# Projections of a four-layer graph network as three fp32r products each, with the head stack in three slots

## The chip, the cores and the metric

One core of one Trainium2 chip runs the whole program. The metric is the device time of one execution in microseconds (us); lower is better. Times come from repeated executions of the same program; the trace comes from one profiled execution.

## The reference, cut to what matters

For each of 32 graphs (512 nodes, 256 features) four residual layers follow one another. Each begins with `h = relu(layernorm(x))`.

```python
# layer 0:  x += silu(rmsnorm((eps*h + adj@h) @ W1 + b1) * w) @ W2 + b2
# layer 1:  hW = h@W + b; att = sigmoid(s1_i + s2_j + c) * adj, masked, rows divided by their sum
#           x += att @ hW
# layer 2:  q, k, v = h@Wq.T, h@Wk.T, h@Wv.T                   (8 heads of 32)
#           scores = q k^T / sqrt(32) + w_head * adj, -inf where adj == 0
#           x += softmax(scores) v @ Wo.T
# layer 3:  x += (D^-1/2 adj D^-1/2) @ (h @ W3) + bias
```

The change concerns the products with Wq, Wk, Wv, Wo (layer 2) and W3 (layer 3), all 256x256, 512 rows per graph.

## The kernel before, in words

`phases(t, tf)` is written once per engine. One round works on two graphs at a time: the front half (layers 0 and 1) of graph `tf = t + 1` and the back half (layers 2 and 3) of graph `t`. So there is a first round with a front half alone, 31 rounds with both halves (t = 0 to 30, 30 of them in a loop), and a last round with a back half alone. The order of the work on each engine is written out by hand; engines meet at semaphores, and each engine runs its list strictly in order, so an instruction that waits holds up all that stands behind it.

Order on TensorE (PE) in a round: `turn(t, 0)` transposes the normed features hb of the back graph (L1059), ACT and DVE copy one half each to bT (L517, L796, both called `turned`); `project_qk(t, 0, 0)` and `(t, 0, 1)` make Q and K of heads 0 to 3 (L1078); `project_v(t, 0)` half of V (L1090); `aggregate(tf)` the adjacency product of layer 0 (L958), which waits for hf, the normed input of the front graph: DVE `stats0` (L667), POOL (L340 to L346), ACT L442. Then `project_v(t, 1)`.

Then follows the grid, g = -4 to 31. At each g PE makes one score tile (L1104 and the mask product L1105, two PSUM banks in turn, so tile i waits for `biased` of tile i-2), the work of the front graph's four node tiles that `tile_steps(g)` says (tile n at its own step u = g + 4 - 8n: `hidden` at u = 0, 1; `turn_hidden` L981 at u = 5, 6; `down` L929 to L931 at u = 11 to 14, all at u = 8 for the last tile), and one group of four transposes of probabilities (L1114). At g = Q1_STEP (0) and K1_STEP (3) stand `project_qk(t, 1, 0)` and `(t, 1, 1)` (heads 4 to 7, into PSUM bank VB, L1078). One step later ACT takes the high part (L526, `qk_high`) and DVE the low part (L801, L621, `qk_low`), both at the end of that step. DVE per step: `bias` (L815), then front work (`hidden` L713 at u = 3, `silu` L719 at u = 4, 5, `hidden_lo` L621 at u = 6, 7), then at g % 4 == 1 a copy (L824). ACT per step: front work (`square` L475 at u = 1, 2, `tanh` L482 at u = 4, 5, `hidden_hi` L430 at u = 6, 7), `exps` (L536), `turned_probs` (L545).

SP copies four pieces per head from qk to a slot of `qk_stack` (`stack`, four slots, L264); head h waits for the scores of head h-4. After the grid: `attend` (L1129); `turn1(tf)` (L1003); `project_o` (L1147), which waits for `attended` on DVE (a copy L838 and a product L841, both into bT); `linear(tf)`; `turn(t, 1)` and again `turned`; `support` (L1154 to L1161, into PSUM, scaled to SBUF by ACT L551 alternating with the sigmoid L512); `attend1(tf)` (L1039, DVE L755 feeds it, `update1` L768 to L777 takes it up); `aggregate3` (L1172), DVE `update3` (L856) into x_out, and SP stores x_out.

A three-product form exists already for W1 and W2: `hi` on ACT rounds a tensor to fp32r (L430), `lo` on DVE subtracts it from the original (L621), and `product` (L926 to L931) issues hi\*hi, hi\*lo, lo\*hi. The projections above are single fp32 matmul calls.

```python
Q1_STEP, K1_STEP = 0, 3                       # L206
if b and g == K1_STEP + 1: qk_low(t, 1, 1)    # DVE; qk_high on ACT likewise
elif u in (4, 5): silu(tf, n, u - 4)          # DVE, after bias(t, g + 4)
```

## Time and profile before

| what | value |
|---|---|
| times of three runs | 4105.31, 4110.77 (median), 4115.6 us |
| span of the profiled execution, first to last instruction | 4105.1 us |
| the profiled execution's own time | not given apart from its span; the fastest run lies 0.2 us above it |
| TensorE clock granted, mean | 0.986 of full speed |
| PE busy 3772.7 us, DVE 2585.8, ACT 2302.1, POOL 688.4 | 92%, 63%, 56%, 17% of the span |

In the trace, an fp32 matmul call appears as two MATMUL rows, an fp32r or bf16 call as one. The duration of a single MATMUL contains its latency, and matmuls overlap, so the cost of one in a stream is the distance between starts. "Idle" in square brackets is time of that engine just before the instruction, and its releaser.

### The profile page before, as it was taken

The page shows a single profiled execution, that of the slowest core. Times are in us where ns is not written, and L with a number is a line of the kernel's source. Part 1 is how long each engine was busy: PE and PEld are TensorE (multiplying, and loading weights), DVE is VectorE, ACT ScalarE, POOL GpSimd, SP SyncE. Part 2 cuts the span into 40 slices and gives each one's busy share as a digit, 9 for nine tenths or more (in the row PEclk, how much of TensorE's full clock was granted, in tenths as well). Part 3 has the DMA queues.
Part 4 walks back from the last instruction along what each step waited for, and adds up shares of the span by engine and source line. Part 5 has one row for each costly group of instructions (what it writes and reads, how often), then busy time and mean ns, then how long its engine had stood idle before and what let it go on. Part 6 is the DMA issues. An engine that isn't in the chain of part 4 may idle for free.

```text
span 4105.1 us, 69147 instructions
## 1 busy us (share of the span) xinstructions
PE 3772.7 (92%) x20364; PEld 2683.0 (65%) x20364; DVE 2585.8 (63%) x6404; ACT 2302.1 (56%) x5155; POOL 688.4 (17%) x1483
## 2 busy tenths in 40 slices
PE   4899999999999999999999999999999999999997
PEld 3666666666666666766666666667666666666674
DVE  3666666666666666666666666666666666666664
ACT  2555565555665555665555655556655556555564
POOL 1121111111111211111121111121111211111110
PEclk9999999999999999999999999999999999999999
DMA  2232222222222322222222223222223222232212
GB/s 73 57 83 62 64 70 61 73 77 67 62 61 62 82 62 68 65 67 66 79 65 62 61 62 82 62 72 61 72 62 82 62 62 61 62 82 66 72 47 62
DMA packets 166933, 275.03 MB, mean 67 GB/s; under 512 B 23906, under 2 KB 59874, under 8 KB 166756
## 3 DMA queue, kind: packets, MB, share of 16 engines
q1 hardware_dynamic: 166756, 273.45, 25.3%
q14 instruction: 161, 1.32, 0.1%
q8 instruction: 16, 0.26, 0.0%
HBM read 122.37 MB, written 16.78 MB: 34 GB/s over the span
## 4 chain that ended last, share of the span: by engine, by line
PE 60%; issue 19%; DVE 11%; ACT 5%; POOL 4%; DVEq 0%; SPq 0%; DMA 0%; POOLq 0%; ACTq 0%
PE turn L1114 9%; PE value L1129 6%; PE front L929 5%; PE front L931 5%; PE front L930 5%; PE score L1104 4%; PE score L1105 4%; PE front L1039 3%; PE front L1024 3%; PE score L1147 3%; PE front L981 3%; POOL small L342 2%; PE score L1161 2%; DVE small L792 2%; DVE hid L719 2%
## 5 line engine op out<-in xcount | busy, mean ns | idle before, releaser
L536 ACT ACTIVATE prob<-prob,small 128x512 f32<-128x512 f32 x1024 | 736.3, 719 | 446.5 <-DVE small L815 445.2
L815 DVE CUSTOM_DVE_ANT_0 prob<-score,adj_sb,drv 128x512 f32<-128x512 f32 x1024 | 761.8, 747 | 250.0 <-PE score L1105 240.4
L1114 PE MATMUL turn<-ident,prob 128*128 128x128 f32 x4096 | 617.2, 276 | 14.1 <-ACT pT L545 8.3
L1114 PEld LDWEIGHTS turn<-ident,prob 128*128 128x128 f32 x4096 | 484.0, 141 | 135.7 <-issue 45.7
L545 ACT ACTIVATE pT<-turn 128x512 f32<-128x512 f32 x768 | 447.1, 585 | 140.7 <-PE turn L1114 140.6
L1104 PE MATMUL score<-qk_stack 128*128 128x512 f32 x1024 | 486.9, 479 | 20.7 <-DVE small L815 19.1
L1105 PE MATMUL score<-unlinked,neg_mask 128*128 128x512 bf16 x1024 | 399.8, 390 | 0.0
L929 PE MATMUL front<-w_hi,s_hi 128*128 128x256 f32 x1024 | 352.2, 344 | 28.5 <-DVE x_in L732 28.5
L442 ACT ACTIVATE hb<-x,small 128x256 f32<-128x256 f32 x256 | 132.8, 589 | 355.7 <-POOL small L346 355.7
L931 PE MATMUL front<-w_hi,s_lo 128*128 128x256 f32 x1024 | 287.4, 281 | 0.0
L930 PE MATMUL front<-w_lo,s_hi 128*128 128x256 f32 x1024 | 286.8, 280 | 0.0
L442 ACT ACTIVATE hf<-x_in,small 128x256 f32<-128x256 f32 x256 | 132.7, 589 | 253.1 <-POOL small L346 253.1
L929 PEld LDWEIGHTS front<-w_hi,s_hi 128*128 128x128 f32 x1024 | 196.5, 192 | 114.1 <-issue 52.6
L713 DVE SCALAR_TENSOR_TENSOR hid<-front,small,rmsw_b 128x512 f32<-128x512 f32 x256 | 180.3, 746 | 121.6 <-POOL small L365 121.6
L958 PE MATMUL front<-adjT_f,hf 128*128 128x512 f32 x512 | 228.2, 599 | 27.5 <-ACT hf L442 27.5
L1129 PE MATMUL value<-pT,vals 128*32 128x512 f32 x2048 | 252.9, 600 | 0.0
L1039 PE MATMUL front<-pT 128*128 128x258 f32 x1024 | 243.5, 389 | 6.3 <-DVE pT L755 1.6
L1078 PE MATMUL score<-bT,ws 128*128 128x512 f32 x256 | 152.4, 751 | 94.3 <-DVE bT L796 93.5
L361 POOL TENSOR_TENSOR small<-small 128x1 f32<-128x1 f32 x128 | 24.9, 195 | 1272.6 <-ACT aside L475 1272.6
L1172 PE MATMUL score<-vals,prob 128*128 128x256 f32 x1024 | 234.6, 382 | 3.3 <-ACT vals L551 0.7
L381 POOL TENSOR_TENSOR inv_x<-small,drv 128x128 f32<-128x128 f32 x256 | 94.9, 403 | 784.6 <-DVE small L831 784.6
L1039 PEld LDWEIGHTS front<-pT 128*128 128x128 f32 x1024 | 189.7, 190 | 54.8 <-DVE x L777 17.6
(137 smaller groups left out, 7515.7 us busy)
## 6 DMA issues: line engine op xcount, KB each, us to landing
qk_stack<-qk SPq DMA_DIRECT2D x1024, 128.0 KB, 2.4
adjT_f<-in_adjT SPq DMA_DIRECT2D x32, 1024.0 KB, 5.4
adj_sb<-in_adj SPq DMA_DIRECT2D x32, 1024.0 KB, 7.9
prob<-in_adjT SPq DMA_DIRECT2D x32, 1024.0 KB, 5.3
x_in<-in_x SPq DMA_DIRECT2D x32, 512.0 KB, 3.5
out<-x_out SPq DMA_DIRECT2D x32, 512.0 KB, 3.0
pT<-in_W SPq DMA_DIRECT2D x2, 1024.0 KB
rmsw_b<-in_rmsw SPq DMA_DIRECT2D x1, 512.0 KB
```

The lines of the kernel that those rows point to most:

```text
L442: act.activation(dst[:, n, :], src[:, n, :], ACT.Relu, bias=nb[:, n:n + 1], scale=rstd[:, n:n + 1]).then_inc(norm["ready"], 1)
L536: act.activation(prob[:, i % 8, :], prob[:, i % 8, :], ACT.Exp, bias=nmax[:, h, n:n + 1], scale=-1.0, accum_out=prsum[:, h, n:n + 1]).then ...
L545: act.activation(pT[:, h % HG, j, :], TB[k % 2][:, :], ACT.Copy).then_inc(pT_act, 1)
L815: dve.tensor_tensor_reduce(out=prob[:, i % 8, :], in0=SB_[i % 2][:, :], in1=adj_sb[:, n, :], scale=neg_w[:, h:h + 1], scalar=3e38, op0=ALU ...
L929: pe.matmul(ps, a[0], b[0], start=start, stop=False)
L930: pe.matmul(ps, a[0], b[1], start=False, stop=False)
L931: return pe.matmul(ps, a[1], b[0], start=False, stop=stop)
L1039: last = pe.matmul(FB[n % 2][:, 0:DE], att[:, m, tile(n)], lin[:, m, :], start=(m == 0), stop=(m == NT - 1))
L1104: pe.matmul(SB_[i % 2][:, :], qk_stack[:, h % 4, 0, tile(n)], qk_stack[:, h % 4, 1, :], start=True, stop=False)
L1105: pe.matmul(SB_[i % 2][:, :], neg_mask[:, h, :], unlinked[:, n, :], start=False, stop=True).then_inc(sc_ps, 1)
L1114: last = pe.transpose(TB[k % 2][:, tile(n)], prob[:, (4 * h + n) % 8, tile(j)], ident[:, :])
L1129: last = pe.matmul(VB[HD * h:HD * h + HD, :], vals[:, j, P * g + HD * h:P * g + HD * h + HD], pT[:, h, j, :], start=(j == 0), stop=(j == N ...
```

## The change

Wq, Wk, Wv, Wo and W3 are held as ws_hi and ws_lo (fp32r), made once at the start. bT becomes bT_hi and bT_lo. `turned` no longer splits the copy between ACT and DVE: ACT rounds both halves, DVE subtracts for both. The attention output is multiplied into a new tile o_f, then rounded by ACT (`attended_high`) and subtracted by DVE (`attended_low`). All products with these operands are three fp32r matmul calls. Q and K of heads 0 to 3 are made in one function that begins when the high part of half 0 is there. To make room, qk_stack has three slots instead of four (head h waits for the scores of head h-3), x_out lies over qk (so `qk_high` of the next graph waits for the store), inv_x and o_f lie over hb, and the widened copy wa is replaced by a broadcast view. Q1_STEP and K1_STEP go from 0 and 3 to 2 and 5. `support` makes its four tiles one after the other.

```diff
         w1_hi, w1_lo = (sb(f"w1_{s}", [P, DT, F], F32R) for s in ("hi", "lo"))
         w2_hi, w2_lo = (sb(f"w2_{s}", [P, FT, D], F32R) for s in ("hi", "lo"))
-        ws = sb("ws", [P, 5, DT, D])
+        ws_hi, ws_lo = (sb(f"ws_{s}", [P, 5, DT, D], F32R) for s in ("hi", "lo"))
         WQ, WK, WV, WO, WG = range(5)
         wl = sb("wl", [P, DT, DE])
-        wa = sb("wa", [P, DT, P])
         b1_rows = sb("b1_rows", [P, F], F32R)
         ones_rows = sb("ones_rows", [P, P], F32R)
         rmsw_b = sb("rmsw_b", [P, F])
...
-        x_out = sb("x_out", [P, NT, D])
         adj_sb = sb("adj_sb", [P, NT, N])
         unlinked = sb("unlinked", [P, NT, N], BF16)
         hb = sb("hb", [P, NT, D])
-        bT = sb("bT", [P, DT, N])
+        bT_hi, bT_lo = (sb(f"bT_{s}", [P, DT, N], F32R) for s in ("hi", "lo"))
         qk = sb("qk", [P, 4, N], F32R)
-        qk_stack = sb("qk_stack", [P, 4, 2, N], F32R)
+        x_out = sb("x_out", [P, NT, D], over="qk")
+        qk_stack = sb("qk_stack", [P, SLOTS, 2, N], F32R)
         vals = sb("vals", [P, NT, D])
         prob = sb("prob", [P, 8, N])
         adjT_b = prob[:, 0:NT, :]
         att = region[:, 0:2048].rearrange("p (m n) -> p m n", m=NT)
         sig = region[:, 2048:3072].rearrange("p (b n) -> p b n", b=2)
         lin = region[:, 3072:3072 + NT * DE].rearrange("p (n d) -> p n d", n=NT)
+        ws_stage = region[:, 5120:7680].rearrange("p (i k n) -> p i k n", i=5, k=DT)
         msg = region[:, 5120:6144].rearrange("p (n d) -> p n d", n=NT)
-        inv_x = sb("inv_x", [P, NT, HG, HD])
+        inv_x = sb("inv_x", [P, NT, HG, HD], over="hb")
+        o_f = sb("o_f", [P, N], over="hb", skip=4 * N)
         small = sb("small", [P, 232])
         def norm_tiles(o):
...
-        freed += [(bT_act, 2, 2), (bT_dve, 2, 2)]
+        freed += [(bT_lo_ready, 4, 3), (bT_lo_ready, 4, 4)]
         assert len(freed) == N_turned and N_turned % 2 == 0
-        SETUP_DVE = 36
+        SETUP_DVE = 35
         def tile_steps(g):
...
             return (u - 11,) if 11 <= u < 15 else ()
         GRID = range(-4, 4 * H)
-        Q1_STEP, K1_STEP = 0, 3
+        STACKED = [64 * len(range(s, H, SLOTS)) for s in range(SLOTS)]
+        Q1_STEP, K1_STEP = 2, 5
         def diag_of(tile):
...
             def stack(t, h):
-                g, s, r = h // HG, h % 4, slice(HD * (h % HG), HD * (h % HG) + HD)
-                if h >= 4:
-                    sp.wait_ge(sc_ps, at(t, 32, 4 * (h - 4) + 4))
+                g, s, r = h // HG, h % SLOTS, slice(HD * (h % HG), HD * (h % HG) + HD)
+                if h >= SLOTS:
+                    sp.wait_ge(sc_ps, at(t, 32, 4 * (h - SLOTS) + 4))
                     unregistered(sp)
                 elif later(t):
                     sp.wait_ge(sc_ps, at(t, 32, 0))
...
             hi(w1_hi[:, :, :], region[:, 0:2048].rearrange("p (k n) -> p k n", k=DT)).then_inc(setup_act, 1)
             hi(w2_hi[:, :, :], region[:, 2048:4096].rearrange("p (k n) -> p k n", k=FT)).then_inc(setup_act, 1)
+            hi(ws_hi[:, :, :, :], ws_stage).then_inc(setup_act, 1)
             act.wait_ge(setup_dve, SETUP_DVE)
...
             def turned(t, i, first):
-                act.wait_ge(b_turned, at(t, N_turned, first + 1))
-                act.activation(bT[:, 0, :], TB[0][:, :], ACT.Copy).then_inc(bT_act, 1)
+                for d in range(DT):
+                    act.wait_ge(b_turned, at(t, N_turned, first + d + 1))
+                    hi(bT_hi[:, d, :], TB[d][:, :]).then_inc(bT_hi_ready, 1)
             def qk_high(t, g, i):
                 act.wait_ge(qk_ps, at(t, 4, 2 * g + i + 1))
+                if g == 0 and i == 0 and later(t):
+                    act.wait_ge(out_stored, t * 16)
                 if g == 1 and i == 0:
-                    for s in range(4):
-                        act.wait_ge(stacked[s], at(t, 128, 64))
+                    for s in range(SLOTS):
+                        act.wait_ge(stacked[s], at(t, STACKED[s], 128 if s == 0 else 64))
                 ps = VB if g else SB_[i]
                 act.activation(qk[:, 2 * i, :], ps[:, :], ACT.Identity,
                                scale=1.0 if i else q_scale[:, g:g + 1]).then_inc(qk_hi_ready, 1)
...
+            def attended_high(t, g):
+                act.wait_ge(o_f_ready, at(t, 2, g + 1))
+                hi(bT_hi[:, g, :], o_f[:, :]).then_inc(o_hi_ready, 1)
             def support(t, n):
                 if n == 0:
...
                         qk_high(t, 1, 0)
                     if b and g == K1_STEP + 1:
                         qk_high(t, 1, 1)
+                    if b and g == 4 * HG + 5:
+                        attended_high(t, 0)
                 if f:
                     layernorm(tf, 1, f_norm, norm_tiles(0), x_in, hf)
+                if b:
+                    attended_high(t, 1)
+                if f:
                     turned1(tf)
                     load_table(tf, 1, ACT.Sigmoid)
                     linear(tf, 0)
...
+            dve.wait_ge(setup_act, 3)
             done(lo(w1_lo[:, :, :], region[:, 0:2048].rearrange("p (k n) -> p k n", k=DT), w1_hi[:, :, :]))
             done(lo(w2_lo[:, :, :], region[:, 2048:4096].rearrange("p (k n) -> p k n", k=FT), w2_hi[:, :, :]))
+            done(lo(ws_lo[:, :, :, :].rearrange("p i k n -> p (i k n)"), region[:, 5120:7680],
+                    ws_hi[:, :, :, :].rearrange("p i k n -> p (i k n)")))
             dve.wait_ge(setup_pe, 1)
             for k in range(DT):
                 done(dve.tensor_copy(wl[:, k, D:DE], FB[k][:, 0:2]))
-                done(dve.tensor_copy(wa[:, k, :], wl[:, k, D + 1:D + 2].to_broadcast([P, P])))
             done(dve.tensor_copy(t2, FB[2][:, 0:2]))
             done(dve.tensor_scalar(s_const, t2[:, 0:1], t2[:, 1:2], cst[:, 17:18], ALU.add, ALU.add))
             assert step[0] == SETUP_DVE, step[0]
...
                 dve.tensor_reduce(deg, adj_sb[:, :, :], AX.X, ALU.add).then_inc(deg_ready, 1)
             def turned(t, i, first):
-                dve.wait_ge(b_turned, at(t, N_turned, first + 2))
-                dve.tensor_copy(bT[:, 1, :], TB[1][:, :]).then_inc(bT_dve, 1)
+                for d in range(DT):
+                    dve.wait_ge(bT_hi_ready, at(t, 4, 2 * i + d + 1))
+                    lo(bT_lo[:, d, :], TB[d][:, :], bT_hi[:, d, :]).then_inc(bT_lo_ready, 1)
             def qk_low(t, g, i):
                 dve.wait_ge(qk_hi_ready, at(t, 4, 2 * g + i + 1))
                 k = turn_of_inv[g]
                 dve.wait_ge(b_turned, at(t, N_turned, k + 1))
-                dve.tensor_copy(bT[:, g, :], TB[k % 2][:, :]).then_inc(lb_ready, 1)
+                dve.tensor_copy(o_f[:, :], TB[k % 2][:, :]).then_inc(lb_ready, 1)
                 dve.wait_ge(lb_ready, at(t, 2, g + 1))
                 dve.wait_ge(av_ps, at(t, 8, 4 * g + 4))
-                dve.tensor_tensor(bT[:, g, :], VB[:, :], bT[:, g, :], ALU.mult).then_inc(o_ready, 1)
+                dve.tensor_tensor(o_f[:, :], VB[:, :], o_f[:, :], ALU.mult).then_inc(o_f_ready, 1)
+            def attended_low(t, g):
+                dve.wait_ge(o_hi_ready, at(t, 2, g + 1))
+                lo(bT_lo[:, g, :], o_f[:, :], bT_hi[:, g, :]).then_inc(o_ready, 1)
             def update2(t):
                 for n in range(NT):
...
                         inverse(t, 1)
                     if b and g == 4 * HG + 4:
                         attended(t, 0)
+                    if b and g == 4 * HG + 6:
+                        attended_low(t, 0)
                 if f:
                     means(tf, 1, f_norm, norm_tiles(0))
                 if b:
                     attended(t, 1)
+                    attended_low(t, 1)
                 if f:
                     turned1(tf)
                 if b:
...
                         if n == NT - 1:
                             ins.then_inc(b_turned, 1)
-            def project_qk(t, g, i):
-                if g == 1:
-                    if i == 0:
-                        pe.wait_ge(v_ready, at(t, 2, 2))
-                    else:
-                        pe.wait_ge(qk_lo_ready, at(t, 4, 3))
-                elif i == 0:
-                    pe.wait_ge(bT_act, at(t, 2, 1))
-                    pe.wait_ge(bT_dve, at(t, 2, 1))
-                    if later(t):
-                        pe.wait_ge(out_ready, at(t, 4, 0))
+            def split(w, k, cols):
+                return ws_hi[:, w, k, cols], ws_lo[:, w, k, cols]
+            def split_bT(k, cols):
+                return bT_hi[:, k, cols], bT_lo[:, k, cols]
+            def project_qk0(t):
+                if later(t):
+                    pe.wait_ge(out_ready, at(t, 4, 0))
                 for k in range(DT):
-                    last = pe.matmul((VB if g else SB_[i])[:, :], ws[:, (WQ, WK)[i], k, tile(g)], bT[:, k, :],
-                                     start=(k == 0), stop=(k == DT - 1))
+                    pe.wait_ge(bT_hi_ready, at(t, 4, k + 1))
+                    for i in range(2):
+                        pe.matmul(SB_[i][:, :], ws_hi[:, (WQ, WK)[i], k, tile(0)], bT_hi[:, k, :], start=(k == 0), stop=False)
+                        pe.matmul(SB_[i][:, :], ws_lo[:, (WQ, WK)[i], k, tile(0)], bT_hi[:, k, :], start=False, stop=False)
+                    pe.wait_ge(bT_lo_ready, at(t, 4, k + 1))
+                    for i in range(2):
+                        last = pe.matmul(SB_[i][:, :], ws_hi[:, (WQ, WK)[i], k, tile(0)], bT_lo[:, k, :],
+                                         start=False, stop=(k == DT - 1))
+                        if k == DT - 1:
+                            last.then_inc(qk_ps, 1)
+            def project_qk1(t, i):
+                if i == 0:
+                    pe.wait_ge(v_ready, at(t, 2, 2))
+                else:
+                    pe.wait_ge(qk_lo_ready, at(t, 4, 3))
+                for k in range(DT):
+                    last = product(VB[:, :], split((WQ, WK)[i], k, tile(1)), split_bT(k, slice(None)), k == 0, k == DT - 1)
                 last.then_inc(qk_ps, 1)
             def project_v(t, j):
                     pe.wait_ge(o_ready, at(t, 2, 0))
                 for i in range(2):
                     for k in range(DT):
-                        last = pe.matmul(VB[:, D * i:D * i + D], bT[:, k, tile(2 * j + i)], ws[:, WV, k, :],
-                                         start=(k == 0), stop=(k == DT - 1))
+                        last = product(VB[:, D * i:D * i + D], split_bT(k, tile(2 * j + i)), split(WV, k, slice(None)),
+                                       k == 0, k == DT - 1)
                 last.then_inc(v_ps, 1)
             def scores(t, i):
                 h, n = divmod(i, NT)
                 if n == 0:
-                    pe.wait_ge(stacked[h % 4], at(t, 128, 64 * (h // 4 + 1)))
+                    pe.wait_ge(stacked[h % SLOTS], at(t, STACKED[h % SLOTS], 64 * (h // SLOTS + 1)))
                 if i == 0:
                     pe.wait_ge(unlinked_ready, at(t, 1, 1))
                     pe.wait_ge(qk_lo_ready, at(t, 4, 2))
                 if i >= 2:
                     pe.wait_ge(biased, at(t, 32, i - 1))
-                pe.matmul(SB_[i % 2][:, :], qk_stack[:, h % 4, 0, tile(n)], qk_stack[:, h % 4, 1, :], start=True, stop=False)
+                pe.matmul(SB_[i % 2][:, :], qk_stack[:, h % SLOTS, 0, tile(n)], qk_stack[:, h % SLOTS, 1, :], start=True, stop=False)
                 pe.matmul(SB_[i % 2][:, :], neg_mask[:, h, :], unlinked[:, n, :],
                           start=False, stop=True).then_inc(sc_ps, 1)
...
                     if n >= 2:
                         pe.wait_ge(x2_ready, at(t, 4, n - 1))
                     for g in range(DT):
-                        last = pe.matmul(SB_[n % 2][:, 0:D], bT[:, g, tile(n)], ws[:, WO, g, :], start=(g == 0), stop=(g == DT - 1))
+                        last = product(SB_[n % 2][:, 0:D], split_bT(g, tile(n)), split(WO, g, slice(None)), g == 0, g == DT - 1)
                     last.then_inc(o_ps, 1)
             def support(t):
-                pe.wait_ge(bT_act, at(t, 2, 2))
-                for n in range(2):
-                    pe.matmul(SB_[n][:, 0:D], bT[:, 0, tile(n)], ws[:, WG, 0, :], start=True, stop=False)
-                pe.wait_ge(bT_dve, at(t, 2, 2))
-                for n in range(2):
-                    pe.matmul(SB_[n][:, 0:D], bT[:, 1, tile(n)], ws[:, WG, 1, :], start=False, stop=True).then_inc(sup_ps, 1)
-                for n in range(2, NT):
-                    pe.wait_ge(sup_ready, at(t, 4, n - 1))
+                pe.wait_ge(bT_hi_ready, at(t, 4, 4))
+                pe.wait_ge(bT_lo_ready, at(t, 4, 4))
+                for n in range(NT):
+                    if n >= 2:
+                        pe.wait_ge(sup_ready, at(t, 4, n - 1))
                     for k in range(DT):
-                        last = pe.matmul(SB_[n % 2][:, 0:D], bT[:, k, tile(n)], ws[:, WG, k, :], start=(k == 0), stop=(k == DT - 1))
+                        last = product(SB_[n % 2][:, 0:D], split_bT(k, tile(n)), split(WG, k, slice(None)), k == 0, k == DT - 1)
                     last.then_inc(sup_ps, 1)
             def aggregate3(t):
...
                     if b and g < 0:
                         scores(t, g + 4)
                     if b and g == Q1_STEP:
-                        project_qk(t, 1, 0)
+                        project_qk1(t, 0)
                     if b and g == K1_STEP:
-                        project_qk(t, 1, 1)
+                        project_qk1(t, 1)
                     if b and g >= 0:
                         turn_probs(t, g // 4, g % 4)
                     if b and g == 4 * HG + 3:
```

## Rows read from the trace of the kernel before

**Rows 1.** The page, busy time of each engine over the span.
```profile
PE 3772.7 (92%) x20364; PEld 2683.0 (65%) x20364; DVE 2585.8 (63%) x6404; ACT 2302.1 (56%) x5155; POOL 688.4 (17%) x1483
```
**Rows 2.** Windows: one round in three stretches; us, busy of PE, PEld, DVE, ACT, POOL, clock, DMA.
```profile
2000.50:2020.50 20.00, 15.98 (x53) 9.09 (x52) 10.39 (x20) 6.09 (x12) 7.19 (x10) 1.00 0.38 91
2020.50:2095.00 74.50, 70.87 (x455) 50.66 (x453) 50.62 (x116) 52.79 (x126) 8.32 (x24) 1.00 0.22 52
2095.00:2125.40 30.40, 29.35 (x137) 23.25 (x134) 19.31 (x63) 12.80 (x24) 6.00 (x12) 1.00 0.27 90
```
**Rows 3.** Timeline of PE: start us, length us, engine, line, operation, count.
```profile
2008.18 1.89 PE L1090 MATMUL value<-ws,bT 128*128 128x256 f32 x8
2011.00 7.13 PE L958 MATMUL front<-adjT_f,hf 128*128 128x512 f32 x16 [0.93 <-ACT hf L442]
...
2020.17 0.39 PE L930 MATMUL front<-w_lo,T_hi 128*128 128x512 f32 x1
2020.40 0.39 PE L931 MATMUL front<-w_hi,T_lo 128*128 128x512 f32 x1
...
2042.73 0.28 PE L929 MATMUL front<-w_hi,s_hi 128*128 128x256 f32 x1
2042.85 0.28 PE L930 MATMUL front<-w_lo,s_hi 128*128 128x256 f32 x1
```
**Rows 4.** Timeline of DVE at the turn of a round.
```profile
2003.72 0.69 DVE L796 COPY bT<-turn 128x512 f32<-128x512 f32 x1 [2.52 <-issue]
2004.33 1.40 DVE L667 BATCH_NORM_STATS2 small<-x_in 128x6 f32<-128x256 f32 x4
```
**Rows 5.** Timeline of ACT at the turn of a round.
```profile
2001.48 0.60 ACT L517 ACTIVATE bT<-turn 128x512 f32<-128x512 f32 x1 [0.90 <-PE turn L1059]
2008.70 2.07 ACT L442 ACTIVATE hf<-x_in,small 128x256 f32<-128x256 f32 x4 [6.62 <-POOL small L346]
```
**Rows 6.** Windows: the first Q and K projection, in two rounds.
```profile
2004.65:2008.30 3.65, 3.65 (x9) 1.74 (x10) 2.51 (x11) 0.00 (x0) 1.92 (x3) 1.00 0.00 0
2129.49:2134.60 5.11, 5.11 (x9) 2.32 (x10) 2.51 (x11) 1.06 (x3) 2.21 (x4) 0.70 0.00 0
```
**Rows 7.** Groups of PE: the first Q and K projection over all rounds.
```profile
L1078 PE MATMUL score<-bT,ws 128*128 128x512 f32 x256 | 152.4, 751 | 94.3 <-DVE bT L796 93.5 <-ACT bT L517 0.8
```
**Rows 8.** Timeline of PE in the grid, and of its first stop.
```profile
2026.30 1.88 PE L1078 MATMUL value<-bT,ws 128*128 128x512 f32 x4
...
2030.39 0.66 PE L981 MATMUL front<-ident,hid 128*128 128x128 f32 x4 [1.31 <-DVE hid L719]
...
2046.65 0.66 PE L981 MATMUL front<-ident,hid 128*128 128x128 f32 x4
```
**Rows 9.** Timeline of DVE in the grid, steps 4 to 8.
```profile
2039.80 0.69 DVE L621 TENSOR_TENSOR qk<-value,qk 128x512 fp32r<-128x512 f32 x1 [2.18 <-ACT qk L526]
...
2043.91 1.41 DVE L713 SCALAR_TENSOR_TENSOR hid<-front,small,rmsw_b 128x512 f32<-128x512 f32 x2 [0.41 <-POOL small L365]
```
**Rows 10.** Timeline of ACT in the grid, step 6 and the copy behind it.
```profile
2042.63 0.73 ACT L536 ACTIVATE prob<-prob,small 128x512 f32<-128x512 f32 x1
...
2043.35 0.58 ACT L545 ACTIVATE pT<-turn 128x512 f32<-128x512 f32 x1
```
**Rows 11.** Timeline of DVE behind the grid: the attention output.
```profile
1970.23 0.69 DVE L841 TENSOR_TENSOR bT<-value,bT 128x512 f32<-128x512 f32 x1 [2.91 <-PE value L1129]
```
**Rows 12.** Timeline of PE behind the grid: output projection and support.
```profile
1971.02 3.67 PE L1147 MATMUL score<-ws,bT 128*128 128x256 f32 x16
...
1981.64 1.13 PE L1154 MATMUL score<-ws,bT 128*128 128x256 f32 x4 [0.58 <-ACT bT L517]
```
**Rows 13.** Timeline of ACT: the second copy of turned features.
```profile
1980.99 0.60 ACT L517 ACTIVATE bT<-turn 128x512 f32<-128x512 f32 x1 [0.28 <-PE turn L1059]
```
**Rows 14.** The page, DMA issues: store of the output.
```profile
out<-x_out SPq DMA_DIRECT2D x32, 512.0 KB, 3.0
```
**Rows 15.** Groups of DVE by shape: the low part of the weights.
```profile
L621 DVE TENSOR_TENSOR w_lo<-pT,w_hi 128x2048 fp32r<-128x2048 f32 x2 | 4.6, 2292 | 0.1
```

33 lines of the change are left out of this document (20 added, 13 removed).

## The prediction, made before the changed kernel was run

> **What bounds the kernel now.** The page's busy line comes first: PE is busy 92% of the span, DVE 63%, ACT 56% [rows 1]. That says "PE", but a mean hides stages, so the next view is one round cut in three windows [rows 2]. In the grid (74.5 us) PE is busy 70.9 of 74.5 us; behind it (30.4 us) 29.4; at the head of the round (20 us) only 16.0. So the grid is a PE stage with short stops, and the head is not. The PE, DVE and ACT timelines then tell what ends each stop:
> - Head. DVE's first instruction of a round comes 2.5 us after its last one with nothing that the profile shows to wait for (2003.72, "issue"), and its normalisation statistics follow at once (2004.33) [rows 4]. POOL and ACT make hf from them by 2010.8 [rows 5], and PE, which had finished its projections, starts `aggregate` 0.93 us late for hf [rows 3]. This chain (DVE, POOL, ACT) decides when `aggregate` starts, not PE.
> - Grid. PE's first stop is 1.31 us before `turn_hidden` of tile 0, for DVE's silu; the Q projection of 1.88 us lies inside the same latency, just before it. By tile 1 (2046.65) there is no stop left: PE's list and the chain square, root mean, `hidden`, tanh, silu end together [rows 8].
> - Behind the grid PE starts `project_o` right when DVE's product for the attention output is done (1970.23 + 0.69, then 1971.02) [rows 11, 12], and `support` when ACT's copy is done (1980.99 + 0.60, then 1981.64) [rows 13, 12]. Both are latencies with hardly any cover.
>
> **What the change takes off PE.** A fp32 call of 256 columns costs 1.72/4 = 0.43 us (four calls as eight rows, 1.89 us less 0.17 of latency, which is a row's length less its distance to the next: 0.39 - 0.23); of 512 columns 6.96/8 = 0.87 us. A fp32r call costs 0.23 us at 512 columns and 0.12 at 256 (distance of starts) [rows 3]. Three of them cost 0.70 and 0.35. So a product gets cheaper by 0.17 us at 512 columns (8 per round) and by 0.08 at 256 (8 each for V, Wo, W3): 1.4 + 1.9 = 3.3 us of PE per round. What counts is where it lies and what is added.
>
> **Part by part, per round with both halves.**
> 1. *Head, `turned`.* DVE now subtracts twice instead of copying once: +0.62 us before its statistics [rows 4]; ACT's two roundings (0.5 us apart) are done before that and cost nothing, since they finish near 2002.6 and DVE comes at 2003.7 [rows 4, 5]. hf, and so `aggregate`, come 0.62 us later. The savings on Q, K and half of V (0.7 + 0.3) lie in front of that wait and are worth nothing. Against it: in most rounds the first Q and K ran partly at the lower of TensorE's two clocks (mean granted 0.70 of full, 5.1 us instead of 3.65) [rows 6]; over all rounds the rows are 751 ns long [rows 7], where full clock gives 0.43 + 0.17 = 0.60 us. Those rounds start `aggregate` some 0.5 us late today and will not after. Taken: +0.3 (bounds 0 and +0.62).
> 2. *Clock.* Today PE stands 3.1 us (4.65 less 1.5, all but the transposes) before Q and K, and what follows that stop is the slow stretch, hidden by the wait for hf. After, PE works through Q, K and V by about 2007.8 and stands 3.8 us until 2011.6; what follows is `aggregate`, which nothing hides. One slow stretch costs 5.1 - 3.65 = 1.5 us [rows 6]. The total excess of rows 7, 0.15 x 256 = 39 us, says it happened in some 25 rounds of 32. Bounds 0 and 1.7; I take +1.2, near the upper one because the stop is longer than today's.
> 3. *`project_v(t, 1)`*: -0.3, on PE's path.
> 4. *Grid, Q1 and K1 moved from steps 0 and 3 to 2 and 5.* Each needs 1.40 instead of 1.72 us. Q at step 0 filled the latency before `turn_hidden` of tile 0; that instruction is tied to DVE's silu, not to PE, so taking Q away only widens the stop. Then Q (+1.40) is behind it, K leaves step 3 (-1.72) and comes back at step 5 (+1.40): PE alone +1.1 us. But K at step 5 also puts `qk_high` and `qk_low` at the end of step 6, ahead of `hidden` of tile 1 in DVE's list. Chain: PE ends K near 2041.9, transposes, score tile 10 ready 2043.0; DVE bias 0.7; ACT exp 0.7 and copy 0.5 [rows 10], then `qk_high` 0.5; DVE `qk_low` 0.7 (it has waited 2.18 us at such a place already, 2039.80, but with nothing urgent behind [rows 9]); bias 0.7; `hidden` 1.33 (today at 2043.91 [rows 9], then 2046.9); bias 0.7, silu 0.6: 2049.6. `turn_hidden` of tile 1 stood at 2046.65 [rows 8]: +3.0. PE meanwhile has only two score tiles, two transposes and 1.4 us of `down`, so it stops for some 2 us. Queued behind on DVE are the biases, for which ACT's exps and PE's transposes wait. Bounds +1.0 (DVE does not block) and +3.5; I take +3.0.
> 5. *Attention output of heads 0 to 3* (steps 20 to 22): one ACT rounding (0.6) and one DVE subtraction (0.7) more; PE is full there, no wait of PE on them before `attend` of the second half. Cover: some 40% of idle ACT and DVE time. +0.2 (0 to 0.5).
> 6. *Behind the grid.* ACT rounding 0.6 and DVE subtraction 0.7 between DVE's product and `project_o`: start +1.3, length -0.7. DVE, which takes x2 up at 0.76 us per tile, now sets the pace: its last statistics +0.7, hb +0.7. At `support` ACT copy and DVE copy side by side become ACT, ACT, DVE, DVE: 0.6 + 0.5 + 0.05 + 0.7 and the hop end at +1.3 on top: start +2.0, first tile +1.2 (all its k at once), from there ACT alternates scaling and sigmoid and DVE's `attention1` follows, so `attend1` and `update1` come +1.2. The whole stage: +1.2 (0.7 to 1.5) [rows 11 to 13].
> 7. *At nothing.* Waits on `out_stored`: the store needs 3.0 us [rows 14] from about 2001.4, `qk_high` comes at 2010.8 at the earliest; cover 6 us. Three slots: head h is copied eight steps ahead instead of twelve; head 4 is ready for copying at 2046.7 and needed four steps later; uncovered it would cost the landing of four pieces. Head 3 waits for head 0's scores, and frees qk long before step 3. The broadcast view of wa costs as its copy did. hb's new tenants meet hb's owner nowhere.
> 8. *Ends.* Subtracting 2560 columns of weights once: 2.9 us by 2292 ns for 2048 [rows 15], less two small copies: +2.4; the rounding is hidden behind DVE's own set-up. Last round, back half alone: about +3.
>
> Sum: 0.3 + 1.2 - 0.3 + 3.0 + 0.2 + 1.2 = 5.6 us in each of 31 rounds = 174, + 5 = 179. The profiled execution spans 4105.1 us and is one of the fast ones (the median of the runs lies 5.7 above): 4105 + 179 = 4284; I say 4285, against the profiled execution, and 4290 against the median lies well inside the range.
>
> **Rivals.**
> - *DVE does not block on `qk_low`* (part 4 is PE work alone, +1.0): 5.6 - 2.0, so 4285 - 62 = 4223. For it: ACT and DVE idle 40%. Against: the list order is strict, and the step order puts the wait there.
> - *The clock does not fall before `aggregate`*: 4285 - 37 = 4248; with the previous one 4186.
> - *The other side: PE's work decides everywhere.* If the 92% were a true bound and each latency had cover, 31 x 3.3 = 102 us come off: 4003. It decides only if hf comes early enough at the head (today it is 0.93 us late [rows 3]) and `project_o` and `support` had other PE work before them. Between the two, an outcome within 0.3%.
> - *Loads not hidden.* Each product has one stationary load more (three calls for two row pairs), 32 per round. If each cost a whole fp32r call of 256 columns, 0.12 us, that is 3.8 us per round: 4285 + 119 = 4404. Against: the 0.12 us between starts at 256 columns already contains a load for each call [rows 3]. By the Trainium skill (TensorE: Matmul & The Clock Gate, "Part 3: Packing small matmuls"), loads overlap running matmuls only across row groups, and all of these use the same ones; its load figure of 128 columns over 1.2 GHz, an estimate of 107 ns each, would make 3.4 us per round. By that rule this trace disagrees: there is no room for it in 0.12 us.
>
> On part 2 the Trainium skill (same page, "Why this matters for your kernels") says that long idle gaps between bursts bring the slow clock back; rows 6 show one such fall here, and by that rule the fall would come in every round, 1.5 instead of 1.2 us.
>
> **Chances.** Forecast 0.50; no block 0.23; no clock fall 0.12; both 0.06; PE decides 0.04; near zero 0.02; loads 0.03. A difference under 0.3% (12 us) is what this measurement cannot tell from nothing. Faster 0.04, same 0.02, slower 0.94. The range takes in the three slower cases and the bounds of parts 2, 4 and 6 on the forecast (upward 0.3 + 0.5 + 0.3 + 0.3 = 1.4 x 31 = 43): 4190 to 4328.
>
> **What would show it.** The page of the changed kernel: PE busy 70 to 110 us lower in a longer span. DVE statistics 0.6 us later after the 2.5 us gap; a stop of 3 to 4 us before L958's successor and a granted clock under 1 in that window in most rounds. `turn_hidden` of tile 1 with a stop of a microsecond or more for DVE, and DVE waiting on ACT's qk before `hidden`. Stops near 1.3 us before `project_o` and 2 us before `support`. Wrong if the grid's length grows by less than 1 us, or if `aggregate` follows V without a stop.

## The result, and the profile after

The changed kernel takes 4360.2 us (4358.96 to 4361.81, four runs), the kernel before 4108.0 in the same measurement (4104.43 to 4115.6, four runs): 1.0613 times as long, 95% interval 1.0601 to 1.0626. The profiled execution spans 4359.0 us, 254 more than before. The direction was forecast, but the time lies above the range.

The page of the changed kernel: the busy line.
```profile
PE 3812.6 (87%) x21388; PEld 2810.8 (64%) x21388; DVE 2656.1 (61%) x6531; ACT 2379.0 (55%) x5284; POOL 699.6 (16%) x1483
```
Against [rows 1], PE's busy time went up by 40 us, although by the prediction's sum its work was cut by 3.3 us in each of 32 rounds. The windows of one round after, in the same three stretches as [rows 2] (us; busy of PE, PEld, DVE, ACT, POOL; granted clock; DMA):
```profile
1990.30:2011.46 21.16, 15.87 (x61) 9.61 (x60) 10.64 (x20) 5.95 (x12) 7.18 (x10) 0.92 0.39 92
2011.46:2087.46 76.00, 70.31 (x431) 53.24 (x429) 50.73 (x118) 52.09 (x124) 8.10 (x22) 0.96 0.17 37
2087.46:2124.00 36.54, 33.09 (x181) 25.55 (x181) 21.07 (x66) 15.98 (x30) 6.59 (x15) 0.95 0.29 101
```
The eye goes to the clock column: 1.00 in all three before; now some of each stretch runs at the lower of TensorE's two clocks (1.2 instead of 2.4 GHz). The boundaries differ slightly from before, so lengths are taken from the next view instead.

The stops of PE in one round, and the rows that follow them, from the timeline of PE after:
```profile
1991.93 0.50 PE L1114 MATMUL score<-bT_hi,ws_hi 128*128 128x512 f32 x1 [0.58 <-ACT bT_hi L443]
...
1994.26 0.73 PE L1118 MATMUL score<-bT_lo,ws_hi 128*128 128x512 f32 x2 [1.14 <-DVE bT_lo L648]
...
2001.39 8.82 PE L995 MATMUL front<-adjT_f,hf 128*128 128x512 f32 x16 [3.57 <-ACT hf L456]
...
2019.66 1.12 PE L1165 MATMUL turn<-ident,prob 128*128 128x128 f32 x4 [1.43 <-ACT prob L554]
2020.43 0.78 PE L1155 MATMUL score<-qk_stack 128*128 128x512 f32 x1
...
2022.14 1.12 PE L1018 MATMUL front<-ident,hid 128*128 128x128 f32 x4 [0.49 <-DVE hid L748]
...
2040.98 0.65 PE L1165 MATMUL turn<-ident,prob 128*128 128x128 f32 x4 [1.92 <-ACT prob L554]
...
2042.65 0.66 PE L1018 MATMUL front<-ident,hid 128*128 128x128 f32 x4
...
2093.30 0.39 PE L966 MATMUL score<-ws_hi,bT_hi 128*128 128x256 f32 x1 [1.18 <-DVE bT_lo L648]
...
2104.85 0.46 PE L966 MATMUL score<-ws_hi,bT_hi 128*128 128x256 f32 x1 [1.99 <-DVE bT_lo L648]
2105.11 0.41 PE L967 MATMUL score<-ws_lo,bT_hi 128*128 128x256 f32 x1
```
The forecast stops are here: 3.6 us before `aggregate`, 1.2 and 2.0 behind the grid, and 1.9 near tile 1, though before the transposes of step 8 (for ACT's exp) and not before `turn_hidden` of tile 1 itself, which has none. What follows them was forecast for one place alone: `aggregate` takes 8.82 us instead of 7.13 [rows 3]. Not forecast are a score matmul 0.78 us long at 2020.43 and 0.41 instead of 0.28 us in `support`. Those are rows at the lower clock, and before there was one such stretch per round at most, at the head and mostly hidden there [rows 6].

DVE and ACT at steps 5 to 7 (timelines of the changed kernel, DVE first):
```profile
2035.42 0.69 DVE L854 COPY pT<-turn 128x512 f32<-128x512 f32 x1 [1.96 <-PE turn L1165]
2036.03 0.75 DVE L845 CUSTOM_DVE_ANT_0 prob<-score,adj_sb,drv 128x512 f32<-128x512 f32 x1
...
2038.64 0.69 DVE L648 TENSOR_TENSOR qk<-value,qk 128x512 fp32r<-128x512 f32 x1 [1.85 <-ACT qk L544]
2039.25 0.74 DVE L845 CUSTOM_DVE_ANT_0 prob<-score,adj_sb,drv 128x512 f32<-128x512 f32 x1
...
2039.92 1.41 DVE L742 SCALAR_TENSOR_TENSOR hid<-front,small,rmsw_b 128x512 f32<-128x512 f32 x2
```
```profile
2037.55 0.58 ACT L563 ACTIVATE pT<-turn 128x512 f32<-128x512 f32 x1
2038.03 0.59 ACT L544 ACTIVATE qk<-value 128x512 fp32r<-128x512 f32 x1
```
`qk_low` of K waits 1.85 us for ACT, and behind it stands `hidden` of tile 1, which now has no wait of its own; before, it stood on POOL's root mean [rows 9].

**Where the time went, by stage.** Mean distances in us between the first rows of each stage in PE's timeline, over the 29 rounds of the loop that lie whole between two rounds like them. "Tn" is `turn_hidden` of tile n.

```text
run            turn   aggr.   first   T0 to  T1 to  T2 to   turn1   linear  turn1' to  attend1  sum
               to     to      hidden  T1     T2     turn1   to      to      attend1    to
               aggr.  hidden  to T0                         linear  turn1'             aggr3
before         10.81   8.44   10.87   16.26  16.63  31.69   4.44    5.49     5.71      7.53    117.9
after          11.13  10.12   10.67   20.27  16.66  31.75   5.28    5.49     6.81      7.64    125.8
```
(turn1': the transposes of `turn(t, 1)`.) The whole stages that are not listed, `aggregate3` and what surrounds it, are the same in both. The difference is 8.0 us per round: +0.32 head, +1.68 `aggregate`, +4.0 between T0 and T1 (less 0.2 before T0), +0.1 in the rest of the grid, +0.84 and +1.10 and +0.1 behind it. 31 such rounds are 247 of the 254 us. (The -0.2 belongs to the products of `project_v(t, 1)`: before the change the row that marks "first hidden" starts 0.2 us early. From the first `w_hi` product to T0 it is 10.4 us in both kernels.)

### The profile page after: what moved, and what is told of

It reads as the page before. It is cut to its first block, busy times and chain, and to the rows that moved or that the text cites. A ratio compares the mean times of both kernels' runs of the same rounds, so it can differ in the third digit from the quotient of the medians.

```text
span 4359.0 us, 71603 instructions
## 1 busy us (share of the span) xinstructions
PE 3812.6 (87%) x21388; PEld 2810.8 (64%) x21388; DVE 2656.1 (61%) x6531; ACT 2379.0 (55%) x5284; POOL 699.6 (16%) x1483
## 4 chain that ended last, share of the span: by engine, by line
PE 57%; issue 20%; DVE 13%; ACT 5%; POOL 4%; DVEq 0%; SPq 0%; DMA 0%; POOLq 0%; ACTq 0%
PE turn L1165 9%; PE value L1180 6%; PE front L966 5%; PE front L968 4%; PE front L967 4%; PE score L1156 4%; PE score L1155 4%; PE front L1018 3%; PE front L1076 3%; PE front L1061 3%; PE score L966 2%; POOL small L355 2%; PE score L967 2%; PE score L968 2%; DVE small L821 2%
## 5 line engine op out<-in xcount | busy, mean ns | idle before, releaser
L1165 PE MATMUL turn<-ident,prob 128*128 128x128 f32 x4096 | 639.9, 283 | 122.2 <-ACT prob L554 113.6
L1165 PEld LDWEIGHTS turn<-ident,prob 128*128 128x128 f32 x4096 | 499.5, 145 | 231.6 <-issue 97.7
L1155 PE MATMUL score<-qk_stack 128*128 128x512 f32 x1024 | 501.4, 493 | 20.2 <-DVE small L845 17.1
L1156 PE MATMUL score<-unlinked,neg_mask 128*128 128x512 bf16 x1024 | 413.6, 404 | 0.0
L995 PE MATMUL front<-adjT_f,hf 128*128 128x512 f32 x512 | 282.5, 716 | 126.3 <-ACT hf L456 126.3
L995 PEld LDWEIGHTS front<-adjT_f,hf 128*128 128x128 f32 x512 | 113.6, 227 | 275.1 <-issue 273.4
L854 DVE COPY pT<-turn 128x512 f32<-128x512 f32 x256 | 176.1, 688 | 139.2 <-PE turn L1165 137.3
L966 PE MATMUL score<-ws_hi,bT_hi 128*128 128x256 f32 x512 | 167.4, 327 | 102.5 <-DVE bT_lo L648 102.5
```

What stands on the lines that cost most here:

```text
L966: pe.matmul(ps, a[0], b[0], start=start, stop=False)
L995: last = pe.matmul(FB[d][:, :], hf[:, m, tile(d)], adjT_f[:, m, :], start=(m == 0), stop=(m == NT - 1))
L1155: pe.matmul(SB_[i % 2][:, :], qk_stack[:, h % SLOTS, 0, tile(n)], qk_stack[:, h % SLOTS, 1, :], start=True, stop=False)
L1156: pe.matmul(SB_[i % 2][:, :], neg_mask[:, h, :], unlinked[:, n, :], start=False, stop=True).then_inc(sc_ps, 1)
L1165: last = pe.transpose(TB[k % 2][:, tile(n)], prob[:, (4 * h + n) % 8, tile(j)], ident[:, :])
```

## The experiments

Theory A: the stops do it, each where the latency of a rounding or a moved projection stands, and each stop brings a slow stretch of the clock with it. Rivals: three slots cannot serve the steps; the roundings as such load ACT and DVE; the clock falls for other reasons. Each kernel was timed beside the kernel before on the same chip; the kernel before had 4111.1 us in the first group, 4109.0 in the second and 4107.7 in the third.

**1. Steps 0 and 3 again (a_q0k3).**
```diff
-        Q1_STEP, K1_STEP = 2, 5
+        Q1_STEP, K1_STEP = 0, 3
```


> The changed kernel with the projections of heads 4 to 7 back at steps 0 and 3; everything else of the change stays, three slots included. Theory A (the move of Q and K out of the latency of tile 0 into the chain of tile 1 costs the grid 3.8 us per round, with the slow clock that the emptied latency brings): the stretch from the first hidden product to turn_hidden of tile 1, 31.0 us in the changed kernel and 27.1 before, falls to about 26.5 (27.1 less two times 0.32 of saved matmul time), so the time is about 4360 - 31 x 4.4 = 4224 us. Rival B (three slots cannot serve steps 0 and 3: the copy of head 3 now waits for head 0's scores, and qk_high at step 1 waits for it): ACT stops some 2 us at step 1 and half or more of the gain is gone, 4290 us or more. Rival C (the extra time in the grid comes from the roundings, not from the move): 4360 within 20.

Measured: 4217.8 us, 1.0251 (1.0227 to 1.0275) of before; T0 to T1 15.93 us instead of 20.27. 142 us of the 252 lie in two constants. The timeline of PE, the same places:
```profile
2216.12 0.65 PE L1018 MATMUL front<-ident,hid 128*128 128x128 f32 x4 [1.36 <-DVE hid L748]
...
2232.07 0.66 PE L1018 MATMUL front<-ident,hid 128*128 128x128 f32 x4
```
No stop before the second one, as in [rows 8], and 15.95 us between them. Rival B falls too: ACT has no idle time before the high part of Q at step 1, and PE waits for a stack copy once in the whole run (2.6 us).

**2. The kernel before at steps 2 and 5 (b_q2k5).**
```diff
-        Q1_STEP, K1_STEP = 0, 3
+        Q1_STEP, K1_STEP = 2, 5
```


> The kernel before, with nothing changed but the two steps: 2 and 5 instead of 0 and 3, four slots, single fp32 calls. Theory A: the move alone costs what it costs in the changed kernel or a little more, since both calls are 0.32 us longer: about +4 us per round, 4108 + 31 x 4.2 = 4238 us. If the move is only PE work shifted behind a stop (my forecast's lower bound, 1.7 us per round with the longer calls): 4160. Rival C (the roundings cost the time, not the move): 4108 within 15.

Measured: 4298.2 us, 1.0453 (1.0435 to 1.0470). The move alone, without a single fp32r product or rounding added, costs 187 us, more than any number I had for it. T0 to T1 is 21.46 us (+5.2), and `aggregate` starts 0.8 us later. Timeline of PE:
```profile
2252.87 1.12 PE L981 MATMUL front<-ident,hid 128*128 128x128 f32 x4 [0.49 <-DVE hid L719]
...
2272.38 0.65 PE L1114 MATMUL turn<-ident,prob 128*128 128x128 f32 x4 [1.93 <-ACT prob L536]
2274.05 0.65 PE L981 MATMUL front<-ident,hid 128*128 128x128 f32 x4
```
The same 1.93 us stop appears, and `turn_hidden` of tile 0 is 1.12 us long instead of 0.66: slow clock. So Rival C is out for the grid. The cost is also above the 4.2 us per round that Theory A had put on it (6.0), with 0.8 of it at the head.

**3. K taken up at step 8 (a_take8).**
```diff
-                    if b and g == K1_STEP + 1:
+                    if b and g == K1_STEP + 3:
                         qk_high(t, 1, 1)
```
(and the same for `qk_low` on DVE.)

> The changed kernel, K still projected by PE at step 5, but its high and low parts taken by ACT and DVE at the end of step 8 instead of step 6, behind DVE's hidden of tile 1. Theory A (qk_low of K holds up hidden of tile 1 in DVE's list, some 2 us of the 3.8): the stretch from the first hidden product to turn_hidden of tile 1 falls from 31.0 to about 29, time 4300 us, if the copy for head 4 (needed at step 12) is still in time. If the hold-up is a story and PE work and the slow clock make it all: 4360 within 15. If the stack gets late: longer than 4360, with PE waiting for the copy at the first score of head 4.

Measured: 4360.9 us, the same as the changed kernel; half a miss. T0 to T1 did fall by 1.94 us (20.27 to 18.33), so the first hidden product to T1 took 29.0 us as expected: the hold-up in DVE's list is real. But T1 to T2 grew by 2.34. The timeline of PE shows with what:
```profile
2043.77 0.66 PE L1018 MATMUL front<-ident,hid 128*128 128x128 f32 x4 [0.68 <-DVE hid L748]
...
2047.02 0.49 PE L1155 MATMUL score<-qk_stack 128*128 128x512 f32 x1 [1.25 <-DMA qk_stack<-qk]
```
1.25 us of it is PE waiting for the copy of head 4, the first of the heads that K at a late step serves. The waits for this copy come in every round with both halves. The other 1.1 us were not taken apart.

**4. The stop before `aggregate` filled (a_fill).**
```diff
                     project_v(t, 0)
+                if b and f:
+                    pe.wait_ge(x1_ready, at(tf, 4, 0))
+                    for _ in range(14):
+                        pe.matmul(FB[0][:, :], w1_hi[:, 0, 0:P], w1_hi[:, 0, 0:N], start=True, stop=True)
```


> The changed kernel with 14 idle fp32r matmuls of 512 columns (0.233 us each, 3.3 us, results overwritten) put between the first half of V and aggregate, where PE stands 3.57 us. Added work, same waits. Theory: aggregate runs at the slow clock only because PE stands before it; with the stop filled it runs in 6.96 us instead of 8.8 on average, and if the granted clock at aggregate is 1.0 in nearly all rounds the time falls by some 31 x 1.8 = 56 us to about 4304, perhaps some more at the start of the grid if the fall there depends on it. Rival (the stop does not decide the clock, or the slow stretch only moves to another place): 4360 within 15, or slower by the overhang of the filler.

Measured: 4288.3 us, 1.0424 (1.0406 to 1.0441): 72 us faster with 14 more matmuls per round. `aggregate` in the groups of PE, first after, then with the filler:
```profile
L995 PE MATMUL front<-adjT_f,hf 128*128 128x512 f32 x512 | 282.5, 716 | 126.3 <-ACT hf L456 126.3
```
```profile
L995 PE MATMUL front<-adjT_f,hf 128*128 128x512 f32 x512 | 229.7, 602 | 31.6 <-ACT hf L456 31.6
```
716 ns against 602 is the slow clock, and the matmuls in place of the idle time (126 us against 32) are all that was changed ahead of it. Aggregate to hidden went from 10.12 to 8.36 us: it was slow in each of the 29 rounds and is so in none now. The rest of the gain, beyond the 56 us expected, is outside `aggregate`: T0 to T1 fell as well, from 20.27 to 19.81. These stages are of the slowest of the four executions (4303.6 us; the others 4282 to 4289).

**5. Q at step 0, K at step 5 (a_q0k5).**
```diff
-        Q1_STEP, K1_STEP = 2, 5
+        Q1_STEP, K1_STEP = 0, 5
```


> The changed kernel with Q of heads 4 to 7 back at step 0 and K left at step 5: splits the 4.4 us per round that both moves cost. K at step 3 or 5 is PE work in the same stretch, so K's move alone should cost only DVE's hold-up, which taking K up later took out of the stretch as 2.0 us: the stretch from turn_hidden of tile 0 to that of tile 1, 15.9 us with both back and 20.3 with both moved, should be 17.9, and the time 4218 + 31 x 2.0 = 4280 us. Then Q's move costs the other 2.4 (1.4 of PE work no longer hidden, 1.0 of slow clock). Rival: the hold-up on DVE exists only because Q is late as well (K waits behind it): 4225 us. Rival: it is all K: 4355.

Measured: 4350.3 us, a miss by 70, and 5 from the rival "it is all K". K's move alone costs 132 us over the run with both at their old steps, Q's then only 10. T0 to T1 grew by 2.9 us, not 2.0, and T1 to T2 by 0.9. PE's timeline:
```profile
2162.73 0.66 PE L1165 MATMUL turn<-ident,prob 128*128 128x128 f32 x4 [1.92 <-ACT prob L554]
2163.14 0.51 PE L1155 MATMUL score<-qk_stack 128*128 128x512 f32 x1
2163.46 0.64 PE L1156 MATMUL score<-unlinked,neg_mask 128*128 128x512 bf16 x1
2163.54 0.77 PE L966 MATMUL front<-w_hi,s_hi 128*128 128x256 f32 x1
```
Behind K's stop the clock is low here (0.64 us for a row that takes 0.39). With Q at step 2 as well, this slow stretch comes earlier, behind the stop at step 0, and not here. Q's 1.43 us in T0 to T1 is thus paid partly by 0.9 us in T1 to T2, and by 0.6 in the stage from turn1' to `attend1`. What each move costs depends on the other.

**6. The stop at step 0 filled (a_fill0).**
```diff
+                    if b and g == 0:
+                        pe.wait_ge(v_ready, at(t, 2, 2))
+                        for _ in range(6):
+                            pe.matmul(VB[:, :], w1_hi[:, 0, 0:P], w1_hi[:, 0, 0:N], start=True, stop=True)
                     if b and g == Q1_STEP:
```


> The changed kernel with six idle fp32r matmuls (1.4 us, results overwritten) at step 0, where Q stood and where PE now stands 1.43 us and then 0.49. Added work, same waits. If the last 1.0 us of the grid's 3.8 per round is the slow clock that follows this stop (transposes at 0.75 us for four instead of 0.42, from 2019.66 on), the stretch from turn_hidden of tile 0 to tile 1 falls from 20.3 to about 19.3 and the time to 4330 us. Rival (the clock falls there for another reason, or the slow rows lie in time that DVE and ACT need anyway): 4360 within 12.

Measured: 4357.6 us, no change. T0 to T1 fell by 0.7 us as the slow stretch left it, but T1 to T2 rose by 0.3, and the stage from turn1' to `attend1` by 0.5. Per round, the time at the lower clock went from 3.8 to 1.0 us in T0 to T1 and from 1.4 to 2.9 behind turn1'. Closing this one stop of several moved slow stretches to another.

**7. Products issued into the two latencies behind the grid (a_tail).**
```diff
             def project_o(t):
+                for n in range(2):
+                    product(SB_[n][:, 0:D], split_bT(0, tile(n)), split(WO, 0, slice(None)), True, False)
+                pe.wait_ge(o_hi_ready, at(t, 2, 2))
+                for n in range(2):
+                    for w in (ws_hi, ws_lo):
+                        pe.matmul(SB_[n][:, 0:D], bT_hi[:, 1, tile(n)], w[:, WO, 1, :], start=False, stop=False)
                 pe.wait_ge(o_ready, at(t, 2, 2))
+                for n in range(2):
+                    pe.matmul(SB_[n][:, 0:D], bT_lo[:, 1, tile(n)], ws_hi[:, WO, 1, :], start=False, stop=True).then_inc(o_ps, 1)
-                for n in range(NT):
+                for n in range(2, NT):
```
(`support` in the same way: high parts of both halves for two tiles, then the low ones.)

> The changed kernel with the order of products in project_o and support alone changed: for the first two tiles, what needs only the earlier half or the high parts is issued while the low part is still being made (the last half's low part comes last). Nothing is added or left out. Theory: the two stops of 1.2 and 2.0 us are latencies of ACT then DVE, so PE work can be put into them: first tile of support 0.5 us earlier, of the output projection 0.5 us earlier, and less room for the slow clock at support: -1.0 to -1.5 us per round, 4315 to 4330 us. Rival (DVE's and ACT's own lists set the pace there, sigmoid and attention1 above all, so a fuller PE changes nothing): 4360 within 12.

Measured: 4340.0 us, 1.0563 (1.0546 to 1.0581). The stages themselves gave 1.66 us per round (5.28 to 4.73, 6.81 to 5.70), as hoped; but `aggregate` to hidden went from 10.12 to 11.14, and the net is 0.6.

**8. DVE's statistics first (a_stats).**
```diff
+                if f:
+                    stats0(tf)
                 if b:
                     turned(t, 0, 0)
                 if f:
-                    stats0(tf)
                     diagonal(tf)
```


> The changed kernel with DVE's statistics of the front graph put ahead of the two subtractions for bT_lo at the head of a round. The chain DVE, POOL, ACT that ends PE's stop before aggregate then starts 1.24 us earlier, while Q and K of heads 0 to 3 end 1.9 us later in the shadow. Theory: aggregate 1.2 us earlier, and with a stop of some 0.5 us instead of 3.6 the clock no longer falls there (1.7 us): about -2.9 us per round, 4270 us. Rival (PE becomes late with Q, K and V instead, and the slow clock falls on them): -0.5 to -1 us per round, 4330 to 4345.

Measured: 4293.1 us, 1.0450 (1.0433 to 1.0468), between the two expectations. `aggregate` to hidden is 8.29 us: full clock. But it starts only 0.2 us earlier, not 1.2, since Q, K and V are now what PE is late with.

**9 to 12. Together (a_combo, a_q0k3_tail, a_combo_fill) and the control (b_stats).** a_combo has the edits of 1, 7 and 8; a_q0k3_tail those of 1 and 7; a_combo_fill those of 1, 7 and 4; b_stats the edit of 8 on the kernel before.

> The changed kernel with three edits together: Q and K back at steps 0 and 3, DVE's statistics ahead of the two subtractions, and products issued into the latencies behind the grid. Nothing added or left out. If the three gains are of different stops they add: from 4218 us (steps alone) less 31 x 2.1 (statistics, as measured) less 31 x 1.7 (the two stops behind the grid, without the slow clock that came back elsewhere) = 4100 us, as fast as the kernel before (4109) or just faster. If slow stretches of the clock move to other stops as they did when one stop was closed alone: 4120 to 4150. All in all the theory says that what is left of the change is then worth next to nothing: its 3.3 us of PE per round against its roundings.

> Steps 0 and 3 and the order behind the grid, without the statistics: 4218 - 31 x 1.7 = 4165 us if the clock behaves as in the run with the steps alone; up to 4200 if aggregate is slow in more rounds than there, as it was when the order behind the grid was changed alone.

> As the previous one (steps, order behind the grid), and with the 14 idle matmuls before aggregate instead of the earlier statistics: it tells how much of a round the slow clock at aggregate still takes. 1.3 us per round at aggregate on average in the run with the steps alone: 4165 - 40 = 4125 us. If it stays above 4150 the slow clock has other places.

> The kernel before with only DVE's statistics put ahead of its copy of bT at the head of a round, to see whether that gain needs the change. There bT comes 1.9 us later, so PE ends Q, K and V(0) at 2012.0 instead of 2010.1 in the coordinates of the profile before, where aggregate starts at 2011.0: about +0.9 us per round, 4137 us, and a stop of 5 us before Q and K, so the slow clock in every round and then +1.5 more, up to 4180. In the changed kernel PE can use the high parts before DVE has come. Rival: hf comes 0.6 us earlier and the round is shorter: 4090.

```text
run            time us   ratio to before     turn to  aggr. to  T0 to  turn1 to  turn1' to
                         (95% interval)      aggr.    hidden    T1     linear    attend1
a_combo        4100.2    0.9983 (0.9974-92)  10.69     8.29     15.93  4.72      5.70
a_q0k3_tail    4166.5    1.0147 (1.0132-63)  11.12    10.02     15.94  4.73      5.70
a_combo_fill   4134.0    1.0068 (1.0055-82)  11.63     8.32     15.94  4.72      5.70
b_stats        4173.8    1.0166 (1.0152-80)  13.08     8.41     16.25  4.44      5.71
```
The first three came within 9 us of the figure that was expected of them, b_stats within 6 us of the upper of its two. a_combo is the best version of all: 260 us under the changed kernel, and 7 us under the kernel before. The interval of that ratio just excludes 1, but 0.2% is less than the 0.3% that the prediction called too small to tell from nothing. With the grid and the rear free of slow stretches, the gains do add. The timeline of PE of a_combo at the head:
```profile
2129.56 1.22 PE L1119 MATMUL score<-bT_lo,ws_hi 128*128 128x512 f32 x2 [2.88 <-DVE bT_lo L648]
...
2134.24 2.31 PE L996 MATMUL front<-adjT_f,hf 128*128 128x512 f32 x5
```
`aggregate` has no stop ahead of it; the 2.9 us stop lies before the low products instead, and the slow rows with it (1.22 us for two against 0.73 above). They are not hidden there, for `aggregate` follows V at once: 4.0 us per round are still at the lower clock, here and in no other stage. The same edit on the kernel before loses 66 us, for there PE cannot begin Q and K until DVE has copied: this gain needs the high parts.

## Why the prediction was wrong

*What held.* The direction, and the mechanism of each stop. Part 1 (head): forecast +0.3 us per round, measured +0.32; the stop before `aggregate` forecast 3.8, measured 3.57. Part 3: -0.3 shows as -0.1 in the `aggregate` stage at full clock (8.3 to 8.4 us against 8.44) and -0.2 before T0. Part 4's chain: `qk_low` before `hidden` of tile 1, a stop of "some 2 us", measured 1.92, one group of transposes earlier than the sign said; experiment 3 took 1.94 us out of that stretch. Part 5: +0.2, measured +0.1. Part 7: neither the store nor the third slot costs a wait in the changed kernel beyond 2.6 us once. Part 8: +5, measured 7 (the 254 us less 247). The rivals "DVE does not block", "the clock does not fall" and "PE's work decides" are refuted by the rows above. "Loads not hidden" too: four V products, twelve fp32r matmuls, take 0.12 us from one start to the next in the changed kernel as well.

*What failed* is three terms of the sum, all too small: 5.6 us per round instead of 8.0. The clock can be taken out of each, because some rounds of other runs have the same stage without any slow stretch. Time at the lower clock in us per round, by stage, mean over the same 29 rounds of each trace:
```text
run       turn to  aggr. to  hidden  T0 to  T1 to  turn1' to
          aggr.    hidden    to T0   T1     T2     attend1
before    2.24     0         0       0      0      0
after     0.28     3.48      1.54    3.77   0.11   1.41
a_fill    0.35     0         0.49    2.13   0.56   1.06
a_fill0   0.16     3.25      0       1.04   0.73   2.94
a_tail    0.77     5.58      2.21    4.10   0.16   0
a_combo   4.00     0         0       0      0      0
```
(The stages left out have none, within 0.02 us.) T0 to T1 as windows of PE (us, busy, count; then granted clock and DMA), first in the changed kernel, then in two rounds of a_fill0:
```profile
2022.14:2042.65 20.51, 18.59 (x100) 0.90 0.09 19
```
```profile
2022.55:2041.64 19.09, 16.69 (x98) 1.00 0.10 21
2154.90:2174.76 19.86, 17.45 (x99) 0.96 0.13 27
```
- Part 2, the clock at `aggregate`: taken +1.2, bound 1.7, measured +1.8 (10.12 us against 8.36 with the stop filled). It was slow in all 29 rounds, where the forecast took some 25 of 32, and by a little more than the 1.5 us of rows 6, where a part of the slow stretch was over before the fp32 rows began.
- Part 4, the grid: taken +3.0, bound 3.5, measured +4.0. The 11 rounds of a_fill and 14 of a_fill0 without a slow stretch in it have 19.09 us from T0 to T1. So PE's share and the hold-up on DVE are +2.8, as forecast, and the other 1.2 us is the slow clock that follows the emptied latency of tile 0. The forecast saw that "taking Q away only widens the stop" and did not ask what a widened stop does to the clock.
- Part 6, behind the grid: taken +1.2, bound 1.5, measured +2.05. 0.45 of it is slow clock at `support`: from `support` to `attend1` it is 3.34 us in the median round and 3.8 in the mean. The other 1.6 is 0.4 more than forecast without any clock. The starts came as forecast (`project_o` +1.3, `support` +2.3 for 2.0), but the output projection got shorter by 0.5 us (3.51 to 3.01), not 0.7; what makes up the rest is open.

So the failed step is the clock as a term: the prediction priced it once, at the longest stop, and put it at nothing behind the other new stops of 1.2 to 2.0 us, without giving a reason. The clock is 3.4 of the 8.0 us (1.8 + 1.2 + 0.45), where 1.2 was taken; everything else is 4.6 us against 4.4 forecast. The granted clock bounds this from outside: its mean is 0.956 over 4359.0 us after and 0.986 over 4105.1 before, at half speed 384 us of low clock against 115. Half of the extra 269 us, 134, is the most that the clock can have cost, and 31 x 3.4 is 105.

One sign failed as well: PE busy was to be 70 to 110 us lower and is 40 higher. Rows at the lower clock are longer, and count as busy.

On the rule of the Trainium skill that the prediction names for part 2 (TensorE: Matmul & The Clock Gate, "Why this matters for your kernels"), which warns against idle gaps between matmul bursts: the trace agrees that the fall comes in every round, and the runs agree in kind, for 14 useless matmuls made the kernel 72 us faster. But slow rows also stood behind stops of 1.4 and 2.0 us here, shorter than the ones that its table warns of.

Was the change itself worth anything? With its steps put back, its statistics first and its stops filled with its own products, it gains at most 0.2% over before. Its 3.3 us of PE per round shrink to 0.3 in the sum of stages (117.9 against 117.6): 0.8 us are gained from the head to T1, and 0.5 lost again from there to `aggregate3`. Two thirds of the work that it makes cheaper lies at the head and rear, where ACT's and DVE's new roundings stand in the way. That these cause the loss is argued from the lists, not tested alone.

## What to carry to other kernels

When a filler is moved out of a latency, price three things: its own work where it lands, what its take-up then holds up in the other engines' lists, and the clock behind the stop that it leaves. Two step constants, changed along with something else, cost here 142 us, more than the 102 us that the whole arithmetic change could earn; a kernel like this one wants them as a run of their own. Where a product of split parts waits for the low part, issue the high products first, into the latency that the split adds; at two places here this took 0.6 and 1.1 us off the stages (a_tail), though only 0.6 us of that 1.7 reached the round while other stops still brought the slow clock.

## What the runs showed of the hardware that was not expected

A slow stretch of TensorE's clock is not bound to one stop. Filling the stop at step 0 took 0.7 us out of one stage and put 0.8 into two others. Shortening the stops behind the grid made the next `aggregate`, 30 to 40 us later, 1.0 us slower: 5.6 us at the lower clock instead of 3.5, and 3.3 instead of 2.6 when the same edit was made with the steps at 0 and 3. With the steps back, the grid has no slow stretch, and the gain of the tail's order came in full (a_q0k3_tail: 51 us, against 20 in a_tail). In a_combo (mean granted clock 0.981) all slow time lies at the head, 4.0 us per round. Each figure by stage is of one profiled execution of its kernel.
